# Relative attention: the bias terms of four heads issued together every second group, and the output bias added to the residual by GpSimd

## The reference, cut to what matters

```
Q = (X @ Wq + bq); K = X @ Wk; V = X @ Wv          # split into 16 heads of 64
R = (X @ Wr + br)                                   # 10 numbers for each token and head
d = t - p; valid = (d >= 0) & (d < 128)
bias = where(valid, 0, -1e9)
extra = einsum('bhtn,ntp->bhtp', R, b_nd[:, d])     # the relative term
logits = einsum('bhtd,bhpd->bhtp', Q, K) / sqrt(64) + bias + extra
W = softmax(logits); A = einsum('bhtp,bhpd->bhtd', W, V)
return A @ Wproj + bproj
```

## Time and profile before

| | |
|---|---|
| median of three runs | 1988.17 us (1985.76 to 1994.25) |
| the profiled execution, its own time | 1986.36 us |
| its span in the profile | 1984.6 us |
| the stage of relative attention | about 947 to 1293 us of the span |
| PE, DVE, ACT, POOL busy, of the whole span | 92%, 74%, 49%, 45% |

### The profile page before, as it was taken

How to read it: one execution, slowest core, us unless ns; L and a number is a source line. 1 busy time by engine, 2 the same in 40 slices (tenths; PEclk the granted TensorE clock), 3 DMA queues, 4 the chain that set the end, 5 groups by cost and what they waited for, 6 DMA issues and landing times. The chain is left out here.

```text
span 1984.6 us, 32861 instructions
## 1 busy us (share of the span) xinstructions
PE 1822.8 (92%) x9946; PEld 1015.8 (51%) x9946; DVE 1469.7 (74%) x4406; ACT 967.4 (49%) x2260; POOL 897.6 (45%) x1307
## 2 busy tenths in 40 slices
PE   5599997699989948897899999989999999999998
PEld 3333333455546633343566666644455555555544
DVE  7488886677747757998477677568877777777788
ACT  4168884477644416340677777733333333334332
POOL 2547771166623311111366677745544456533341
PEclk8679998699989968998999999999999999999999
DMA  8552224444450039961654465311221442423211
GB/s 283 155 122 40 38 24 75 107 109 85 111 109 22 23 83 148 158 139 51 168 173 150 148 175 156 96 60 47 77 76 56 130 136 81 144 77 109 63 32 32
DMA packets 240450, 201.86 MB, mean 102 GB/s; under 512 B 26868, under 2 KB 222874, under 8 KB 239640
## 3 DMA queue, kind: packets, MB, share of 16 engines
q1 hardware_dynamic: 222472, 171.36, 34.7%
q0 software_dynamic: 17376, 28.29, 5.7%
q10 hardware_dynamic: 432, 0.10, 0.0%
HBM read 116.80 MB, written 82.89 MB: 101 GB/s over the span
## 5 line engine op out<-in xcount | busy, mean ns | idle before, releaser
L2868 DVE SCALAR_TENSOR_TENSOR x<-f_m,f_gs,x 128x128 f32<-128x128 f32 x1024 | 304.5, 343 | 60.8 <-PE f_m L2693 54.8
L515 DVE TENSOR_REDUCE a_nmax<-a_s 128x1 f32<-128x512 f32 (+3 forms) x512 | 276.3, 584 | 80.9 <-PE a_s L321 33.2
L2236 POOL TENSOR_SCALAR a_lg<-a_lg,a_rinv 128x256 f32<-128x256 f32 (+1 forms) x256 | 225.3, 897 | 151.8 <-DVE a_rinv L2273 151.3
L2693 PE MATMUL f_m<-f_wo,f_oT 128*128 128x512 f32 x512 | 248.2, 595 | 0.9
L2641 POOL DMA_INDIRECT f_yg<-yslot,slot x160 | 152.2, 951 | 190.6 <-PE f_s L2727 104.2
L432 ACT ACTIVATE a_pT<-a_st 128x512 f32<-128x512 f32 (+3 forms) x512 | 227.2, 520 | 19.3 <-issue 6.4
L318 PE MATMUL a_s<-t_kp,t_qp 96*128 96x512 bf16 (+3 forms) x512 | 164.2, 355 | 13.3 <-DVEq L499 12.4
L341 PE MATMUL a_st<-t_qp,t_kp 99*128 99x512 bf16 (+3 forms) x512 | 161.5, 351 | 2.2 <-ACT a_pT L432 1.5
L2693 PEld LDWEIGHTS f_m<-f_wo,f_oT 128*128 128x128 f32 x512 | 95.9, 190 | 125.8 <-issue 110.2
L2821 ACT COPY f_pT<-f_t 128x512 f32<-128x512 f32 x128 | 75.2, 587 | 170.5 <-PE f_t L2735 113.7
L2868 DVE SCALAR_TENSOR_TENSOR f_val<-f_m,gate,f_val 128x128 f32<-128x128 f32 x336 | 113.1, 343 | 40.7 <-PE f_m L2693 26.9
(11 more groups left out here) (429 smaller groups left out, 3814.5 us busy)
## 6 DMA issues: line engine op xcount, KB each, us to landing
a_band<-band SPq DMA_DIRECT2D x64, 512.0 KB, 4.4
band<-s_hole SPq DMA_DIRECT2D x16, 1032.0 KB
band<-a_rows SPq DMA_DIRECT2D x64, 256.0 KB, 4.1
yslot<-f_ys SPq DMA_DIRECT2D x45, 256.0 KB
f_xs<-spare_rows SPq DMA_DIRECT2D x9, 832.0 KB
w_gate_up<-f_wgu_in SPq DMA_DIRECT2D x4, 1536.0 KB, 14.4
t_qp<-parts SPq DMA_DIRECT2D x192, 32.0 KB
t_kp<-parts SPq DMA_DIRECT2D x192, 32.0 KB
```

The lines of the kernel that those rows point to most:

```text
L515: v.tensor_reduce(nmax[:, h % 4, qt:qt + 1], s_ps[(b * H * QT + u) % R][:, 0:n], AX.X, ALU.max, negate=True)\
L2236: last = pool.tensor_scalar(lg[:, g % 2, half, p, c0:c0 + n], lg[:, g % 2, half, p, c0:c0 + n], rinv[:, g % 2, p, qt:qt + 1], None, ALU.mult)
L2693: pe.matmul(ps[:, :], left, w, start=True, stop=True).then_inc(full, 1)
L2868: ins = v.scalar_tensor_tensor(out, ps[:, e * P:(e + 1) * P], gate, out, ALU.mult, ALU.add)
```

## The change

Three things change in the stage. First, the terms of four heads, a quad, are issued together, in every even group, on four strips of rows and into four banks. Second, `relative_rows` moves to the odd groups; `order`, ACT's program, and SP's stores (now four after each other in every even group) follow. The first groups get eight heads' terms and a third `relative_rows` ahead of the loop instead of six and two. Third, the output bias is no longer a product: its row is loaded into all 128 partitions, POOL adds it to the residual `x` of each batch at the start of the stage, and DVE, ahead of adding a batch's result to `x`, waits for that.

```diff
-               ("wv", [P, 2, 512]), ("wo", [P, 8, P]), ("bq", [P, 8]), ("bo", [1, P]), ("scale", [P, 1]))
+               ("wv", [P, 2, 512]), ("wo", [P, 8, P]), ("bq", [P, 8]), ("bo", [P, P]), ("scale", [P, 1]))
...
-    return [(k.a3[name], d[f"a3_{name}"]) for name, _ in sources]
+    return [(k.a3[name], bc(d["a3_bo"], [P, P]) if name == "bo" else d[f"a3_{name}"]) for name, _ in sources]
...
     def terms_at(g):
 
-        names = [("e", 2 * (g + AHEAD)), ("e", 2 * (g + AHEAD) + 1)] if g + AHEAD < G else []
-        return names + ([("r", g // 2 + 2)] if g % 2 == 0 and g // 2 + 2 < QUADS else [])
-
-    order = [("r", 0), ("e", 0), ("e", 1), ("q", 0), ("k", 0), ("r", 1), ("e", 2), ("e", 3), ("e", 4), ("e", 5)]
+        if g % 2 == 0:
+            return [("e", 4 * (g // 2 + 2) + j) for j in range(4)] if g // 2 + 2 < QUADS else []
+        return [("r", (g + 5) // 2)] if (g + 5) // 2 < QUADS else []
+
+    order = [("r", 0), ("e", 0), ("e", 1), ("e", 2), ("e", 3), ("q", 0), ("k", 0), ("r", 1)]
+    order += [("e", i) for i in range(4, 8)] + [("r", 2)]
...
-            for i in range(4, 6):
+            for i in range(4, 8):
                 store(i)
...
-                if g + 1 < G:
-                    store(2 * g + 2)
-                    store(2 * g + 3)
+                if g % 2 == 0 and g // 2 + 1 < QUADS:
+                    for i in range(2 * g + 4, 2 * g + 8):
+                        store(i)
...
-            def relative_terms(i):
-                names = [("e", i), ("e", i + 1)]
-                if i % 4 == 0:
-                    emptied(("r", i // 4))
-                banks = [opened(name) for name in names]
+            def relative_terms(m):
+                emptied(("r", m))
+                banks = [opened(("e", 4 * m + j)) for j in range(4)]
                 for qt in range(QT):
-                    for (_, j), (ps, full) in zip(names, banks):
-                        r = slice(32 * (j % 4), 32 * (j % 4) + NR)
-                        last = pe.matmul(ps[:, qt * P:(qt + 1) * P], rT[r, i // 4 % 2, qt * P:(qt + 1) * P], buckets[r, :],
+                    for j, (ps, full) in enumerate(banks):
+                        r = slice(32 * j, 32 * j + NR)
+                        last = pe.matmul(ps[:, qt * P:(qt + 1) * P], rT[r, m % 2, qt * P:(qt + 1) * P], buckets[r, :],
                                          start=True, stop=True)
...
                 if c == C - 1:
-                    for qt in range(QT):
-                        last = pe.matmul(y_ps[:, qt * P:(qt + 1) * P], k.ones[0:1, :], bo[:, :], start=False,
-                                         stop=True, skip_group_check=True)
                     last.then_inc(y_full, 1)
...
-            relative_terms(2)
-            relative_terms(4)
+            relative_terms(1)
+            relative_rows(2)
...
-                if g + AHEAD < G:
-                    relative_terms(2 * (g + AHEAD))
                 if g % 2 == 0 and g // 2 + 2 < QUADS:
-                    relative_rows(g // 2 + 2)
+                    relative_terms(g // 2 + 2)
+                if g % 2 == 1 and (g + 5) // 2 < QUADS:
+                    relative_rows((g + 5) // 2)
...
         @block.gpsimd
         def _(pool):
+            pool.wait_ge(k.a3_in, 16 * len(k.a3))
+            for b in range(B):
+                xs = k.x[:, b * QT:(b + 1) * QT, :]
+                pool.tensor_tensor(xs, xs, bc(bo[:, :].unsqueeze(1), [P, QT, P]), ALU.add).then_inc(x_biased, 1)
...
                     v.wait_ge(y_full, b + 1)
+                    v.wait_ge(x_biased, b + 1)
                     xs = k.x[:, b * QT:(b + 1) * QT, :]
```

More of the change, by code:

```diff
@@ L1884, in relative_heads @@
     V_ORDER = (0, 2, 4, 6, 1, 3, 5, 7)
-    NR, AHEAD, QUADS = 10, 3, B * 4
+    NR, QUADS, RB = 10, B * 4, 4
     HF, E, GATE, BEST = 8, 8, 21, 7
@@ L1951, in relative_heads @@
         rT = ph.sb("rT", [P, 2, T])
-        rows = ph.sb("rows", [P, 4, QT, P])
+        rows = ph.sb("rows", [P, RB, QT, P])
         work = ph.sb("work", [P, 2, HF * 64])
@@ L1969, in relative_heads @@
         gates, logits = (t[:, 0:NT * P].rearrange("p (i s c) -> p i s c", s=2, c=64) for t in (k.gate, k.logits))
-        exp_done, rinv_ready, scaled, pv_done, o_read, y_full, y_read, spare_set = (
+        exp_done, rinv_ready, scaled, pv_done, o_read, y_full, y_read, spare_set, x_biased = (
             ph.sem(s) for s in ("exp_done", "rinv_ready", "scaled", "pv_done", "o_read",
-                                "y_full", "y_read", "spare_set"))
+                                "y_full", "y_read", "spare_set", "x_biased"))
         block = ctx.enter_context(nc.Block())
@@ L2114, in out_products @@
                 for qt in range(QT):
-                    pe.matmul(y_ps[:, qt * P:(qt + 1) * P], oT[:, g % 2, qt * P:(qt + 1) * P], wo[:, c, :],
-                              start=(c == 0 and qt == 0), stop=False, skip_group_check=True)
+                    last = pe.matmul(y_ps[:, qt * P:(qt + 1) * P], oT[:, g % 2, qt * P:(qt + 1) * P], wo[:, c, :],
+                                     start=(c == 0 and qt == 0), stop=(c == C - 1), skip_group_check=True)
                 if c == C - 1:
-                    for qt in range(QT):
-                        last = pe.matmul(y_ps[:, qt * P:(qt + 1) * P], k.ones[0:1, :], bo[:, :], start=False,
-                                         stop=True, skip_group_check=True)
                     last.then_inc(y_full, 1)
@@ L2197, in _ @@
             term("r", 0)
-            term("e", 0)
-            term("e", 1)
+            for i in range(4):
+                term("e", i)
             keys(0)
             term("r", 1)
-            for i in range(2, 6):
+            for i in range(4, 8):
                 term("e", i)
+            term("r", 2)
             for g in range(G + 1):
```

## The result

| | before | changed |
|---|---|---|
| median, first comparison (6 runs each) | 1990.38 us | 1976.05 us (1967.03 to 1978.25) |
| ratio, 95% interval | | 0.9915 (0.9886 to 0.9944) |
| median, second comparison (11 and 6 runs, one chip) | 1994.09 us | 1976.11 us (1967.91 to 1980.14) |
| ratio, 95% interval | | 0.9902 (0.9873 to 0.9932) |
| profiled execution, span | 1986.36, 1984.6 us | 1978.25, 1976.4 us |

What follows compares the result with a forecast made beforehand. PE was taken to bound the stage, issuing without a gap. Gains of 8.8 (pairs), 3.6 (groups 24 to 28), 2.5 (bias) and 1.1 (end) sum to 16.0 us: 1988.2 - 16.0 = 1972.2 us, range 1965 to 1980.

Steps and rivals of the forecast that it cites:

- block of four heads: PE's products of terms in an even group: four heads at once cost what a block of two costs, 1.09 us.
- slot of four strips: On PE, one pass of 128 columns on four strips of rows side by side: taken as 0.11 us.
- even group: Steady stage: 10.30 us instead of 10.73, its end set by ACT's four copies ahead of the next `scores`.
- groups 24 to 28: Late groups that make no values: 44.9 us against 48.53, 3.6 us gained, with group 25's bias in it.
- end of the stage: Path to the next stage, where DVE waits for the last bias product: shorter by some 1.1 us.
- first two groups and what is ahead of them: Stage's start: first band up to 1 us earlier, `scores(1)` up to 1 us later; counted 0, from -2 to +2.
- new wait: Even groups: `scores` opens all four banks and waits for ACT's fourth copy of the terms, 0.48 us.
- Rival B: ACT reaches the terms early enough or copies faster, so its waits go: 7.9 us more gained, 1964.3 us; chance 0.05.
- C: Terms on PE: four strips run as two and two, slot 0.22 us; 10.4 of the gain goes, 1982.6; chance 0.10.
- C': Terms on PE: a slot between, 0.14 us, costs 0.15 more in 13 groups, 1974.2 us; chance 0.07.
- D: Terms on PE: weight loads share one path, strips go one at a time, slot 0.44 us; slower, 2005; chance 0.04.
- E: Steady pairs: PE no longer ahead, DVE adds waits where it works on gates; 5 us, 1977; chance 0.04.

## Why the prediction was right

The forecast was 1972.2 us and a gain of 16.0; measured were 1976.1 twice, inside the range, and gains of 14.3 and 18.0, on both sides of it. The forecast's time is 4 us low, for the most part because it started from a median of three runs, 1988.2; with more runs the kernel before stands at 1990.4 and 1994.1. By the stage, whose scatter is small, each step can be set beside its term:

| step | forecast | measured |
|---|---|---|
| block of four heads | as long as one of two, 1.09 | 1.11 us |
| slot of four strips | 0.11 | 0.112, as with two |
| even group | 10.30 | 10.33 |
| odd group | 9.45 | 9.44 |
| groups 24 to 28 | 44.9 | 44.9 |
| groups 2 to 28, bias included | -14.9 | -14.7 |
| end of the stage | -1.1 | -1.05 |
| first two groups and what is ahead of them | 0 (-2 to +2) | +0.6, +1.0 |

The bound named was the right one: PE issued without a gap, so each block taken away was gained in full until ACT's copies came last. That new wait was the forecast's main step, and it is there: the even group is ACT's path and not PE's, and ends 0.15 us behind the fourth copy. Its price was set too high. Without it the forecast had 9.82, so 0.48 a group; the runs without it have 9.98, so it cost 0.35. The difference is the keys' bank: it delays PE's own path by 0.15, under the wait, where it doesn't count. The forecast had put it at 0.04 and added it behind ACT's copies, on the path where it doesn't lie. What lengthened that path was that ACT began its copies 8.12 us after the group's start (1196.76 - 1188.64) and not 8.07. That 10.30 came within 0.03 of 10.33 is in this part luck.

The Trainium skill, page "TensorEngine Tiling (Array Packing)", section Performance Considerations, says that tiling doesn't speed up the emptying of PSUM. The trace agrees: behind the block that was made denser PE waits for ACT, 5.4 us in the stage. Opening the banks by halves gave back 5.5 us in the steady part: 11 times 0.35, and twice 0.98 in groups 24 and 26, less 0.3 that group 27 is then longer. Rival B, which had no wait, had priced it at 7.9.

The start: DVE's first minimum began 968.49 - 955.32 = 13.2 us after the first product, where before it was 14.9 (13 to 15 in the profiles with four heads at a time, 15 to 16 in those with two), so the stores of four heads together did help, by 1.8 us where the forecast had "up to 1 us" (and named over 2 us as a sign of being wrong). But `scores(0)` now waited behind ACT, and ACT behind the stores. The changed kernel in order of time, ACT, PE and DVE:

```profile
966.81 1.32 ACT L2190 ACTIVATE a_rows<-a_m 128x512 f32<-128x512 f32 x2 [0.91 <-DMA band<-a_rows]
...
967.56 1.79 PE L2080 MATMUL a_m<-a_kT,a_qT 64*128 64x128 f32 x16 [1.69 <-ACT a_rows L2190]
...
968.49 0.29 DVE L2268 CUSTOM_DVE_ANT_0 a_lg<-a_m,a_band 128x128 f32<-128x128 f32 x1 [7.12 <-DMA a_band<-band]
```

This wait was not in the forecast's working. The trace names the band as what DVE waited for, but the minimum began 0.93 us after these scores, and in group 23 it begins 0.94 after them (1199.91 - 1198.97) with no wait for a band. So the late scores can have held it as well; which of the two came last is open. From the first product to group 2 the three profiles with two heads at a time took 34.1, 35.6 and 35.7 us and those with four 33.2 to 35.6, so the start's sign is not settled.

Rivals C and C' fell with the slot: four strips keep 0.11. D fell with it. (The 0.9 us that the forecast named as the sign is eight slots alone; up to the next work the block takes 1.11.) E fell: in the changed kernel no pair between 2 and 23 is longer than another, apart from the counting in group 13, and the list of waits has PE behind DVE for 0.8 us in all. A page of the Trainium skill, "TensorE: Matmul & The Clock Gate", section "Measured speedup vs the span model", gives 3.07 for four row tiles of 512 columns. The slot of about 0.145 that the prediction made of it didn't appear: at 128 columns it is 0.112 with four strips as with two. No run here issues one strip at a time, so the speedup over a single one isn't measured.

The two profiled executions, taken alone, would have shown half the gain. The forecast had said that the median and the profile stood 1.8 us apart; it had not said that the time ahead of the stage moves by 9 us between executions.

## What to carry to other kernels

When a block on the bounding engine is made denser, count when its results are emptied: here four results came at once, and the work behind them asked for all four banks before its first product. Asking for a buffer where it is first used, rather than at the head of a routine, is a one-line edit that gave back 5.5 us, over a third of what the whole change had gained. And when the rest of a program scatters by more than the change is worth, compare the changed stage by itself, and in it the part behind its start: the steady part of two kernels that were profiled twice repeated to 0.02 and 0.05 us and their whole stage to 0.4 and 0.6, where runs of one kernel differ by 10 and more.

## What was not expected

Pairs of strips don't wait for each other: in the block of two pairs issued one behind the other, the second pair began 0.33 us before the first pair's last record, and the block took 1.65 us where 16 slots of 0.112 and the way in and out would be 2.0. Why it began after five slots of eight, and not earlier, was not tested. POOL's additions of 128x512 took 1.23 us each (4.93 for four), while DVE had nothing to do, not the 1.85 of the slowest row; another of POOL's additions of this size in the kernel before took 1.27, so the slowest row was too high a price. What makes it slower there was not tested.
